# A Mamba layer between two feed-forward stages on one core: GpSimd's ring of u products has six places in place of four

## What is computed

```python
x = x + 0.5 * ffn(layernorm(x))      # coupling network, three cycles
x = x + mamba(layernorm(x))
x = x + 0.5 * ffn(layernorm(x))      # the same weights
```

```python
x = silu(conv(xn @ in_w)); delta = softplus(x @ wd1 @ wd2 + b)
Bm, Cm = x @ wB, x @ wC
h[e, n] = exp(delta[e] * A[e, n]) * h[e, n] + (delta[e] * x[e]) * Bm[n]
y[e] = sum_n h[e, n] * Cm[n]
out = resid + ((y + W_D * x) * silu(skip)) @ out_w
```

## Time and profile before

| | us |
|---|---|
| median of 3 runs | 1316.61 (1315.49 to 1316.68) |
| the profiled execution | 1316.35 |
| its span on the core | 1314.6 |
| busy in the span: TensorE | 1090.7 (83%) |
| VectorE | 1162.0 (88%) |
| ScalarE | 760.6 (58%) |
| GpSimd | 853.1 (65%) |

### The profile page before, as it was taken

How to read it: one execution, slowest core, us unless ns; L and a number is a source line. 1 busy time by engine, 2 the same in 40 slices (tenths; PEclk the granted TensorE clock), 3 DMA queues, 4 the chain that set the end, 5 groups by cost and what they waited for, 6 DMA issues and landing times. The chain is left out here.

```text
span 1314.6 us, 11061 instructions
## 1 busy us (share of the span) xinstructions
PE 1090.7 (83%) x2800; PEld 479.5 (36%) x2800; DVE 1162.0 (88%) x1727; ACT 760.6 (58%) x1298; POOL 853.1 (65%) x374
## 2 busy tenths in 40 slices
PE   3999747779898789979879998987998867799973
PEld 2444213333353343335334333533433423443421
DVE  3765899998999999899999989999999999676587
ACT  2656658757545756754674584467466444266665
POOL 0000003989999989989998998999899999000000
PEclk9999988889999999999999989989999989999998
DMA  6000003344544445444454434544444453000003
GB/s 208 1 1 1 1 1 114 129 141 148 154 134 161 152 137 161 154 136 161 138 159 153 160 130 128 169 153 161 129 159 156 145 181 112 0 1 1 1 1 129
DMA packets 48000, 146.57 MB, mean 111 GB/s; under 512 B 5504, under 2 KB 14336, under 8 KB 47936
## 3 DMA queue, kind: packets, MB, share of 16 engines
q1 hardware_dynamic: 47440, 145.03, 33.4%
q10 hardware_dynamic: 496, 0.82, 0.2%
HBM read 141.05 MB, written 4.72 MB: 111 GB/s over the span
## 5 line engine op out<-in xcount | busy, mean ns | idle before, releaser
L1174 POOL TENSOR_TENSOR late<-m_dx,m_brow 128x1024 f32<-128x1024 f32 x256 | 596.6, 2354 | 20.2 <-DVE m_a_bank L1303 20.1
L970 ACT ACTIVATE m_a_bank<-m_delta,m_negA 128x512 f32<-128x512 f32 x512 | 334.5, 683 | 165.8 <-DVE m_hc L1315 127.3
L1480 PE MATMUL m_y_bank<-m_hc,ident 128*128 128x512 f32 x640 | 326.1, 634 | 85.8 <-DVE m_hc L1315 85.8
L1186 POOL TENSOR_TENSOR m_hc_pool<-m_hid,m_crow 128x1024 f32<-128x1024 f32 x96 | 225.7, 2351 | 25.1 <-DVE m_hid L1303 24.7
L1480 PEld LDWEIGHTS m_y_bank<-m_hc,ident 128*128 128x128 f32 x640 | 122.0, 200 | 264.2 <-issue 133.4
L1315 DVE TENSOR_TENSOR m_hc<-m_a_bank,m_crow 128x512 f32<-128x512 f32 x320 | 203.0, 676 | 0.0
L1303 DVE TENSOR_TENSOR_SCAN m_a_bank<-m_a_bank,m_carry,late 128x512 f32<-128x512 f32 x160 | 196.2, 1273 | 2.7 <-ACT m_a_bank L970 2.7
L1303 DVE TENSOR_TENSOR_SCAN m_a_bank<-m_a_bank,late 128x512 f32<-128x512 f32 x160 | 186.5, 1211 | 3.6 <-ACT m_a_bank L970 3.6
L1480 PE MATMUL m_y_bank<-m_hc_pool,ident 128*128 128x512 f32 x384 | 183.6, 601 | 0.0
L1195 POOL TENSOR_TENSOR m_dx<-m_delta,m_x 128x1024 f32<-128x1024 f32 x16 | 37.7, 2354 | 217.2 <-ACT m_delta L1075 217.2
L1303 DVE TENSOR_TENSOR_SCAN m_hid<-m_a_bank,m_carry,late 128x512 f32<-128x512 f32 x96 | 117.7, 1268 | 10.4 <-ACT m_a_bank L970 10.4
(11 more groups left out here) (156 smaller groups left out, 1300.6 us busy)
## 6 DMA issues: line engine op xcount, KB each, us to landing
m_brow<-bc_rows SPq DMA_DIRECT2D x128, 512.0 KB, 4.9
m_crow<-bc_rows SPq DMA_DIRECT2D x128, 512.0 KB, 4.0
x_tok<-x_in SPq DMA_DIRECT2D x4, 1024.0 KB, 8.5
out<-x_tok SPq DMA_DIRECT2D x3, 1024.0 KB, 4.4
w<-w_in SPq DMA_DIRECT2D x1, 1024.0 KB, 12.0
out<-x_tok SPq DMA_DIRECT2D x4, 256.0 KB, 2.1
w<-w_in SPq DMA_DIRECT2D x1, 750.0 KB, 10.3
w<-w_in ACTq DMA_DIRECT2D x1, 512.0 KB, 5.8
```

The lines of the kernel that those rows point to most:

```text
L970: nc.scalar.activation(a_bank[K % 2][:, j, :], delta[:, i % 2, c, :], ACT.Exp, scale=negA[:, c, n:n + 1]).then_inc(S["a"], 1)
L1174: nc.gpsimd.tensor_tensor(u[:, K % U_RING, :, :], dx[:, i % 2, 2 * q:2 * q + 2, :], brow[:, K // 2 % ROW_RING, K % 2, :].unsqueeze(1).to_b ...
L1186: nc.gpsimd.tensor_tensor(hc_pool[:, before % POOL_RING, :, :], hid[:, before % POOL_RING, :, :], crow[:, K // 2 % ROW_RING, K % 2, :].uns ...
L1480: op = nc.tensor.matmul(y_bank[:, j, :], ident[:, :], source[:, before % ring, j, :], start=False, stop=K % PASS == PASS - 1)
```

## The change

The ring of u has six places; the buffer grows from 4 to 6 places of 2 x 512 elements in each partition; the reserve in SBUF for descriptors of DMAs that GpSimd would issue goes from 8192 to 4096 bytes. Each engine has the same instructions in the same order before and after. Only the waits of `drive` for a scan differ: scan K - 6 in place of K - 4.

```diff
-    U_RING, ROW_RING, HC_RING, POOL_RING = 4, 3, 3, 2
+    U_RING, ROW_RING, HC_RING, POOL_RING = 6, 3, 3, 2
...
-            "late": sb("late", [P, 4, 2, BANK]),
+            "late": sb("late", [P, 6, 2, BANK]),
...
-    nc = bacc.Bacc("TRN2", target_bir_lowering=False, num_devices=1, dynamic_dma_scratch_size=8192)
+    nc = bacc.Bacc("TRN2", target_bir_lowering=False, num_devices=1, dynamic_dma_scratch_size=4096)
```

## The result

| | before | six places |
|---|---|---|
| median of 20 runs each, us | 1316.64 | 1319.66 |
| fastest and slowest | 1313.67, 1320.56 | 1317.48, 1324.95 |
| ratio | | 1.0025, 95% interval 1.0015 to 1.0035 |
| the profiled execution (its span) | 1316.35 (1314.6) | 1324.95 (1323.2) |

The change costs 3.3 us by the ratio, with an interval of 2.0 to 4.6 us (3.0 us between the medians). The 0.2% that a measurement can tell from no change, 2.6 us, lies inside this interval: it is a real cost, at the edge of what shows. The profiled execution of the changed kernel was its slowest of 20, 8.6 us longer than that of before, so the two traces show more than the mean difference of 3.3 us.

What follows compares the result with a forecast made beforehand. VectorE's stream was taken to bound the kernel. The profiled 1316.35 us plus 2.31 for one product gave 1318.66; from the median, 1316.61 + 2.31 = 1318.9 us (+0.18%), other terms 0; range 1315.2 to 1321.2.

Steps and rivals of the forecast that it cites:

- What bounds the kernel: Scan stage: VectorE's own stream sets the end; GpSimd keeps up and VectorE never waits for it.
- The mechanism and its place: At L1235, the full ring's pause at 269.61 us ended VectorE's longest block; six places move the end to about 271.9.
- The size: At the second half's small norm steps: one more GpSimd product, +2.31 us, bounded by 0 and 4.6 us.
- The first ring wait that lasts is the one at 269.61, so both kernels do the same until then: Start of the scan stage: claimed no difference between four and six places before unit 15's product.
- the term of +2.31 us: VectorE's small norm steps around L1235: held until 271.9 us, one GpSimd product longer, none of it coming back.
- within 0.2%, close below its edge: Whole kernel: predicted +0.18% against a 0.2% (2.6 us) measuring limit; chance of staying within it 0.61.
- the weighing's wait excludes the second: Behind unit 15's product, GpSimd must pause for unit 12's weighing, so 2.31 us was taken, not 4.6.
- Three runs lie within 1.2 us, so they seem to fall alike: TensorE's clock drops: an argument against rival (a), that drops fall alike from run to run.
- Rival (a): Slower: the hold plus a TensorE clock drop at the second feed-forward stage's start, about 1.7 us more, 1320.6; chance 0.32.
- Rival (b): Small steps get in at ends of GpSimd instructions, so the ring ends no block; time stays 1316.6; chance 0.13.
- Rival (c): Faster: GpSimd is the hidden bound of the scan stage, freed waits reach VectorE, 1313.9 us; chance 0.07.
- The terms taken as 0: Buffer addresses, b and c row transfers, the halved descriptor reserve and GpSimd's other ring waits: each claimed to cost 0.

Runs made afterwards that it cites:

- u4_wide: Ring of four places as in the kernel before, but with the buffer of six and the halved descriptor reserve; 1315.93 us, ratio 1.0002.
- after: The changed kernel with six places, against the four of the kernel before; median 1319.66 us, ratio 1.0025, profiled execution 1324.95 us.
- after_again: The changed kernel with six places, run once more for a second profile; 1325.16 us, one execution.
- u4_six_at_two: Buffer of six places; GpSimd waits for scan K - 6 at units 10 and 15, K - 4 elsewhere; 1319.16 us, ratio 1.0017 to the kernel before.
- u6_more: Six places plus fourteen added VectorE steps with two SBUF operands and unused results; 1355.18 us, ratio 1.0289 to the kernel before.
- u4_gps: Four places; two-operand norm steps of the second half moved to GpSimd, VectorE keeping the two reciprocals; 1308.52 us, ratio 0.9943 to the kernel before.

## Why the prediction was right, and where it wasn't

**What bounds the kernel: right.** VectorE's stream sets the end, GpSimd's freed waits moved to the weighings, and VectorE's waits for ScalarE shifted along.

**The mechanism and its place: right.** The ring's wait is what ended the block, and a deeper ring makes the block longer by one product: 5.82 to 8.10 us at L1235 in the short way, 7.82 to 10.19 at L1226 in the long. The cost vanishes when no step is held, and it follows the two waits at units 10 and 15.

**The size: right for one way only.** The step that doesn't hold in general is "The first ring wait that lasts is the one at 269.61, so both kernels do the same until then". That holds for the execution I had read, a short one. On the long way L1226 is held to a pause as well, and there too the ring decides when it comes: with four places its wait at 252.74 in `u4_wide` lasts 2.64 us. So the term of +2.31 us was right for one way (2.28 measured) and should have been two products, 4.5 us, for the other. By these two prices the 3.3 us measured would be a mixture with (3.3 - 2.3)/(4.5 - 2.3), roughly 45%, on the long way. This share is worked out, not counted. The interval of 2.0 to 4.6 us allows any share from none to all. The working also supposes the same share before and after, which isn't shown: the profiles with six places at both units (`after`, `after_again`, `u4_six_at_two`, `u6_more`) all went the long way, of the five with fewer only `u4_wide`. The predicted 1318.9 stands against 1319.66, and a forecast "within 0.2%, close below its edge" against a result at that edge. That it came so near is partly luck: the one execution read had gone the short way, and 2.31 lies inside the measured interval although other executions pay more.

**The argument that excluded a second product** ("the weighing's wait excludes the second") was right at one place and overlooked that there are two places.

**"Three runs lie within 1.2 us, so they seem to fall alike"** was weak: 20 runs of the same kernel spread over 6.9 us, and most of that is the hold, since the 24 executions of the four kernels without it lie within 3.2 us.

**Rival (a)**, slower, had the right sign and the wrong cause: beyond unit 11 nothing was added, and no fall of the clock is needed. **Rival (b)**, no longer block: refuted by the ratio, by the depth at units 10 and 15 and by the fourteen steps. The Trainium skill (SBUF — State Buffer, practical consequences), as the prediction reads it, has VectorE held for one GpSimd instruction at most. The runs bear that out in 12 of 14 extra steps, and go against it in the ones held for up to 10 us. **Rival (c)**, faster: refuted; four and six places are alike once the hold is gone.

The terms taken as 0 (addresses, rows, reserve, other ring waits) show nothing together: 1.0002 for the addresses and the reserve, and with six places 0.8 and 0.4 us less than with four in the two pairs without the hold, which is within the noise.

## What to carry to other kernels

Look for instructions of a size that can't explain their length; a 128x16 step of 5.8 us in the bounding engine's stream was worth more than the ring's two extra places. Where two engines contend for SBUF, a buffer that lets the one run on without a pause takes away the other's openings, so more slack can cost time. Then move the small step to the other engine, which kept the whole computation here and gained 7 us. One operand in place of two isn't a cure by itself: the reciprocals were never held, the tensor_scalar was. And don't judge the size of a hold by one execution.

## What the runs showed of the hardware

- A held VectorE step gets in either at the first end of a GpSimd instruction or only when GpSimd pauses: 5.82 us across two ends, 7.82 and 8.48 across three, 10.19 across four. Which of the two it will be isn't settled; both come at the same step with four places (0.98 us before, 7.82 in `u4_wide`).
- A step with one SBUF operand can be held too: L1239, a tensor_scalar of 128x16, took 2.38 us with GpSimd busy, 0.16 us with it idle (269.65, before) and 0.16 us where GpSimd changed instructions (273.79, `u4_six_at_two`). Reciprocals of the same shape took 0.19 to 0.25 us in every run, beside a busy GpSimd too.
- GpSimd does such steps in 0.21 to 0.27 us (`u4_gps`), while its own products of 128x1024 take 2.35.
